# Layers 2 and 3: bonus and level 0 in one product set, narrow tiles for levels 4 and 5, the 512 to 160 projection token by token

## The chip, the cores and the metric

The kernel runs on one core of a Trainium2 chip. The metric is the device time of one execution in microseconds, lower is better; a time shown without more is the median of several executions. Engines are named as in the profile: PE (TensorE), PEld (its weight loads), DVE (VectorE), ACT (ScalarE), POOL (GpSimd), SP (SyncE, which only issues transfers here).

## The reference

Four cross-attention layers run one after the other over 16 batch items of 128 tokens with 512 channels, all in float32. Layer 0 is attention with 64 inner channels, layer 1 a latent attention with an MLP of 2048, layer 2 a block of the RWKV kind, layer 3 grouped-query attention with a layer norm. The change is in layers 2 and 3, nearly all of it in the first half of layer 2:

```python
xa = _ln(x, ln1_w, ln1_b)
sx = shifted(xa) - xa
xxx = jnp.tanh((xa + sx * maa_x) @ maa_w1).reshape(b, l, 5, DM)      # 512 -> 160
xxx = jnp.einsum('blfd,fde->blfe', xxx, maa_w2)
xm = xa[:, :, None] + sx[:, :, None] * (maa_stack + xxx)             # five mixes: k, w, v, r, g
w = jnp.exp(-jnp.exp(time_decay + jnp.tanh(xw @ td_w1) @ td_w2))
r, k, v, g = xr @ Wr.T, xk @ Wk.T, xv @ Wv.T, silu(xg @ Wg.T)
def step(s, rkvw):                     # one head: 16 x 16 state, 32 heads, token by token
    a = k_t[..., :, None] * v_t[..., None, :]
    out = jnp.einsum('bhi,bhij->bhj', r_t, u * a + s)                # u: the bonus
    s = a + w_t[..., :, None] * s
```

## The kernel before

Each layer is written engine by engine, with semaphores set by hand. Layers 2 and 3 are `layers23`. The work on one batch item is cut into five stages, n, p, w, a and b (first layer norm; the recurrence; the rest of layer 2; attention; last layer norm), and in one turn of the loop each stage works on another item, so that a turn holds one item's work of every stage. `ORDER` lists, for each engine, the steps of a turn in the order in which that engine takes them: an engine goes through its list strictly, and a step whose semaphore isn't there yet holds all that is behind it. The first four turns and the last four run with part of the stages. TensorE's list is unrolled, the others are loops. The engines' steps have the same names; on TensorE `p_mix` multiplies, on ScalarE, VectorE and GpSimd `p_xm` finishes each mix.

The recurrence is done in levels. The scores between a token and the tokens before it are built by doubling: for the level `lv` with n = 2^lv, the tokens of an odd block of n meet the keys of the even block ahead of it. `p_diag` makes the products of each token with itself, with the bonus u in `ur` (L1433). `p_level(lv)` (L1624 to L1643) makes the level's products: for 4 channel chunks, 2 halves of the tokens and 4 row groups of 32 channels (two heads) one matmul with K2 (64 keys, each with an even-head and an odd-head column, so 128 weight columns) as weights and 32 tokens of rT as moved operand. Every float32 matmul is two records in the profile, a transpose one. VectorE merges the level into AD under a mask (`p_merge`, L2095) and multiplies the odd tokens of rT by their decay (`p_rup`, L2085), GpSimd multiplies the even keys (`p_kup`, L1445), both with the products of decays that `p_wl` made. Each level claims the four banks "quad", which the merge before it frees, and waits for its rup and kup. `p_s0`, `p_av` and `p_av6` then weigh the values.

The projection from 512 to 160 (`p_t5`, L1541 and L1543) has the channels of maa_w1 as weights and 128 tokens moved: four matmuls for the first 128 outputs, four for the other 32. Its tanh (t5, t5b) feeds `p_mix` (L1555, four mixes, each on its own row group and bank of quad) and `p_mix4` (L1564, the fifth, on row group 0, into bank 7). `p_g` leaves tanh and value in two tiles; `out` has a tile of its own.

PSUM banks are claimed through `Use`: a step on TensorE waits until the step before it on that bank has been emptied. `USES` says which step has which bank (quad, 5, 6 or 7).

Of the kernel before, what the change touches and what calls it, by code (L numbers as in the profile page):

```python
# [447 lines left out]
def layer1(nc, a, PS, sem, C, R, cols_of, ident, halfs, bn_scale, bn_shift, l0_out, l1_out, weights, early,  # L448
# [15 lines left out]
    with ExitStack() as ctx:  # L464
# [63 lines left out]
        with nc.Block() as block:  # L528
            @block.sync
            def _(sp):  # L530
# [526 lines left out]
def layers23(nc, a, PS, quad, sem, C, R, CS, col_at, ident, hsum, halfs, l1_out, early, s_early):  # L1057
# [6 lines left out]
    SETUP = 12  # L1064
    LAT = [0, 32, 48, 56, 60, 62]
    NLM = 64

    with ExitStack() as ctx:
# [6 lines left out]
        def chunked(t):  # L1075
# [23 lines left out]
        t5 = sb("t5", [P, P])  # L1099
        t5b = sb("t5b", [DM, P])  # L1100
# [4 lines left out]
        ur = sb("r_bonus", [P, NC, P])  # L1105
# [5 lines left out]
        AD6 = xmix[:, 0:2, :, :].rearrange("p f c t -> p (f c t)").rearrange("p (n t) -> p n t", t=HALF)  # L1111
# [3 lines left out]
        zg = sb("gate_tanh", [P, D])  # L1115
# [42 lines left out]
        out = sb("out3", [P, D])  # L1158
        wvm = out[:, 0:P].rearrange("p (c m h) -> p c m h", c=NC, m=NC)
# [36 lines left out]
        s_gate = sem("p_silu_ready")  # L1196
# [29 lines left out]
        USES = {("n_xa",): (6, 1), ("p_t5",): (6, 1), ("p_mix",): ("quad", RG), ("p_mix4",): (7, 1), ("p_u1",): (5, 1), ("p_w",):  # L1226
                (6, 1), ("p_k",): (5, 1), ("p_r",): (6, 1), ("p_v",): (5, 1), ("p_g",): (7, 1), ("p_diag",): ("quad", 1),
                ("p_level", 0): ("quad", 1), ("p_level", 1): ("quad", 1), ("p_level", 2): ("quad", 1), ("p_level", 3): ("quad", 1),
                ("p_level", 4): ("quad", 1), ("p_level", 5): ("quad", 1), ("p_level", 6): ("quad", 1), ("p_s0",): (7, 1),
                ("w_var",): (7, 1), ("w_rstd",): (6, 1), ("w_out",): (7, 1), ("w_xc",): (6, 1), ("w_fk",): (6, 1), ("w_fr",): (7,  # L1230
                1), ("w_fv",): (5, 1), ("a_x",): (5, 1), ("a_q",): (5, 1), ("a_kv",): (6, 1), ("a_score", 0): ("quad", RG),
                ("a_score", 1): ("quad", RG), ("a_turn", 0): (6, 1), ("a_turn", 1): (5, 1), ("a_turn", 2): (5, 1), ("a_turn", 3):
                (6, 1), ("a_turn", 4): (6, 1), ("a_turn", 5): (7, 1), ("a_turn", 6): (5, 1), ("a_turn", 7): (5, 1), ("a_norm",): (7,
                1), ("b_out",): (7, 1)}
# [3 lines left out]
            pe=[("p_t5",), ("a_x",), ("w_var",), ("p_mix",), ("a_kv",), ("b_out",), ("a_q",), ("p_mix4",), ("w_rstd",), ("a_score",  # L1238
                0), ("p_k",), ("p_r",), ("a_score", 1), ("p_u1",), ("a_turn", 0), ("w_out",), ("a_turn", 1), ("p_w",), ("p_diag",),
                ("a_turn", 2), ("p_g",), ("p_level", 0), ("w_xc",), ("p_v",), ("a_turn", 3), ("p_level", 1), ("w_fr",), ("p_level",  # L1240
                2), ("n_xa",), ("a_value", 0), ("a_turn", 6), ("p_level", 3), ("w_fk",), ("p_level", 4), ("a_turn", 5), ("a_turn",
                7), ("a_turn", 4), ("a_norm",), ("p_level", 5), ("w_fv",), ("p_level", 6), ("a_value", 1), ("p_s0",), ("p_av",),
                ("p_av6",)],
            act=[("p_t5",), ("a_x",), ("p_xm", 0), ("p_xm", 3), ("p_xm", 1), ("a_kv",), ("p_xm", 2), ("a_q",), ("w_rstd",), ("p_xm",
                 4), ("p_k",), ("a_exp", 0), ("p_r",), ("a_exp", 1), ("p_u1",), ("a_exp", 2), ("a_turn", 0), ("a_turn", 1),
                 ("a_exp", 3), ("a_turn", 2), ("p_w",), ("p_g",), ("w_xc",), ("a_exp", 6), ("a_exp", 5), ("a_turn", 3), ("p_v",),
                 ("a_exp", 4), ("a_exp", 7), ("n_xa",), ("w_fr",), ("a_turn", 6), ("w_fk",), ("a_turn", 5), ("a_turn", 7),
                 ("a_turn", 4), ("a_norm",), ("b_store",), ("p_level6",), ("a_bias",), ("p_wkv",)],
# [1148 lines left out]
```

## Time and profile before

| | |
|---|---|
| median of 3 runs | 2489.3 us (2488.08 to 2489.41) |
| the profiled execution, its time | 2494.95 us |
| its span, first to last instruction | 2492.6 us |
| mean granted TensorE clock | 0.966 |
| busy | PE 2331.0, PEld 1720.1, DVE 1111.1, ACT 1082.6, POOL 552.4 us |
| layers 0 and 1 | until about 1200 us |
| layers 2 and 3 | from about 1200 us on |

Busy times are from one execution. PE's count the tail of each matmul, so they say who is full, not how near the engine is to its peak; what a group of matmuls costs is read from its start and the start of the next group.

### The profile page before, as it was taken

Reading aid. Unit: us, or ns where it says so; the run is one execution under the profiler, and the core shown is the slowest. Engines: PE = TensorE matmul, PEld = TensorE weight load, DVE = VectorE, ACT = ScalarE, POOL = GpSimd, SP = SyncE. Lnnn points to the kernel's source line nnn. Section 1 sums busy time; section 2 is a strip of 40 time slices with the busy share of each in tenths; the row PEclk is TensorE's granted clock in tenths of the full one; section 3 lists DMA queues with packets and bytes.
Section 4 is the critical chain, followed back from the end, with each engine's and each line's share of the span. In section 5 each row is a group of like instructions: output and inputs, shape, how many; then the busy total and the mean of one; then the engine's idle time right before and its main releaser. Section 6 shows DMA issues by size and latency. Waiting matters only on the chain. (4 is left out here: it accounts for less than half of the span.)

```text
span 2492.6 us, 59022 instructions
## 1 busy us (share of the span) xinstructions
PE 2331.0 (94%) x22880; PEld 1720.1 (69%) x22880; DVE 1111.1 (45%) x3070; ACT 1082.6 (43%) x3409; POOL 552.4 (22%) x585
## 2 busy tenths in 40 slices
PE   7886999999999999999488999999999999999986
PEld 3444667777777666667276878777777877777864
DVE  5662222222222222222234565655666655665542
ACT  4552333333333333333112655555555455555544
POOL 0001010110000000000023334333333343343320
PEclk9997999999999999999678999999999999999998
DMA  5421000000000000000600000111000011100010
GB/s 165 168 89 65 15 18 18 22 18 18 18 18 18 18 18 18 18 10 5 191 15 16 21 17 14 25 25 25 20 20 12 23 25 25 25 20 16 10 25 14
DMA packets 117056, 81.93 MB, mean 33 GB/s; under 512 B 79136, under 2 KB 91680, under 8 KB 114720
## 3 DMA queue, kind: packets, MB, share of 16 engines
q1 hardware_dynamic: 107744, 54.32, 8.2%
q0 software_dynamic: 2240, 12.58, 1.5%
q10 hardware_dynamic: 6912, 12.59, 1.3%
q8 instruction: 138, 2.26, 0.4%
q14 instruction: 22, 0.18, 0.0%
HBM read 62.68 MB, written 12.58 MB: 30 GB/s over the span
## 5 line engine op out<-in xcount | busy, mean ns | idle before, releaser
L745 PEld LDWEIGHTS bank<-normedT,mlp_w 128*128 128x128 f32 x2048 | 235.7, 193 | 18.3 <-issue 17.1
L745 PE MATMUL bank<-normedT,mlp_w 128*128 128x128 f32 x2048 | 241.7, 278 | 0.8 <-DVE normedT L975 0.8
L755 PE MATMUL bank<-mlp_w,geluT 128*128 128x512 f32 x512 | 228.9, 595 | 0.0
L1638 PEld LDWEIGHTS quad<-rT,k_even_odd 32*128 32x128 f32 x6144 | 187.2, 193 | 39.5 <-DVE wkv_scores L2095 29.7
L926 DVE CUSTOM_DVE_ANT_0 probs<-quad,neg_mask 128x256 f32<-128x256 f32 x256 | 90.8, 421 | 273.8 <-PE quad L675 273.8
L1638 PE MATMUL quad<-rT,k_even_odd 32*128 32x32 f32 x6144 | 197.9, 278 | 13.9 <-DVE wkv_scores L2095 11.5
L2095 DVE COPY_PREDICATED wkv_scores<-level_masks,quad 128x1024 f32<-128x1024 int32 x96 | 160.6, 1673 | 93.4 <-PE quad L1638 93.4
L1930 ACT ACTIVATE scores<-scores,nmax 128x128 f32<-128x128 f32 x512 | 198.9, 400 | 2.9 <-DVE nmax L2185 2.9
L933 DVE COPY probsT<-quad 128x512 f32<-128x512 f32 x128 | 84.9, 683 | 191.9 <-PE quad L689 191.7
L755 PEld LDWEIGHTS bank<-mlp_w,geluT 128*128 128x128 f32 x512 | 93.6, 190 | 103.4 <-issue 103.4
L1445 POOL TENSOR_TENSOR k_even_odd<-k_even_odd,decay_products 128x512 f32<-128x512 f32 x80 | 95.9, 1199 | 275.9 <-PE quad L1638 275.9
L861 ACT ACTIVATE geluT<-bank,cols 128x128 f32<-128x128 f32 x256 | 73.3, 369 | 178.2 <-PE bank L745 178.2
L2085 DVE TENSOR_TENSOR rT<-rT,decay_products 128x256 f32<-128x256 f32 x96 | 61.9, 645 | 160.4 <-PE quad L1638 123.4
L869 ACT ACTIVATE probs<-probs,nmax 128x256 f32<-128x256 f32 x256 | 126.6, 498 | 2.6 <-DVE nmax L926 2.4
L1386 POOL TENSOR_TENSOR gn_rstd<-gn_var_eps,halfs 128x32 f32<-128x32 f32 x16 | 87.1, 5443 | 159.1 <-DVE gn_var_eps L2110 159.1
L2185 DVE CUSTOM_DVE_ANT_0 scores<-quad,mask 128x128 f32<-128x128 f32 x512 | 112.7, 287 | 21.5 <-PE quad L1748 20.8
L1402 POOL TENSOR_TENSOR xm<-xm,xaT 128x512 f32<-128x512 f32 x80 | 101.1, 1264 | 77.4 <-DVE xm L2053 77.4
L647 PE MATMUL quad<-hT,k_w 128*128 128x256 f32 x512 | 113.2, 379 | 0.0
L656 PE MATMUL quad<-v_w,hT 128*128 128x512 f32 x256 | 112.5, 592 | 0.0
L579 POOL COPY rinv_repeated<-rinv 128x256 f32<-128x256 f32 x32 | 12.8, 399 | 439.2 <-DVE rinv L939 439.2
L1939 ACT ACTIVATE probsT<-bank 128x512 f32<-128x512 f32 x128 | 73.0, 597 | 75.6 <-PE bank L1505 75.6
L647 PEld LDWEIGHTS quad<-hT,k_w 128*128 128x128 f32 x512 | 96.1, 190 | 12.4
(238 smaller groups left out, 4463.7 us busy)
## 6 DMA issues: line engine op xcount, KB each, us to landing
x_in<-in_x SPq DMA_DIRECT2D x32, 256.0 KB, 3.0
mlp_w<-in_mlp_w POOLq DMA_DIRECT2D x8, 1024.0 KB, 5.5
ctx_in<-in_ctx SPq DMA_DIRECT2D x16, 256.0 KB, 2.9
l_out<-wy ACTq DMA_DIRECT2D x16, 256.0 KB, 2.2
wy_in<-l_out SPq DMA_DIRECT2D x16, 256.0 KB, 3.4
hT<-in_ctxT SPq DMA_DIRECT2D x16, 256.0 KB, 3.5
l_out<-l_x ACTq DMA_DIRECT2D x16, 256.0 KB, 2.0
x_in<-l_out SPq DMA_DIRECT2D x16, 256.0 KB, 3.0
```

The costliest lines, as they stand in the source:

```text
L647: mm = nc.tensor.matmul(PS[b][:, e * 256:(e + 1) * 256], k_w[:, c, m * P:(m + 1) * P], hT[:, c, :], start=(c == 0), stop=(c == NC - 1))
L656: mm = nc.tensor.matmul(PS[b][:, :], hT[:, c, n * P:(n + 1) * P], v_w[:, c, :], start=(c == 0), stop=(c == NC - 1))
L745: mm = nc.tensor.matmul(PS[b][:, f * P:(f + 1) * P], mlp_w1[:, c, m * P:(m + 1) * P], nT[:, c, :], start=(c == 0), stop=(c == NC - 1))
L755: mm = nc.tensor.matmul(PS[M.bank][:, :], gT[:, f, :], mlp_w2[:, f, :], start=(f == 0), stop=(f == NF - 1))
L869: ac = nc.scalar.activation(probs[:, h, :], probs[:, h, :], ACT.Exp, bias=nmax[:, h:h + 1], scale=-1.0, accum_out=rsum[:, h:h + 1])
L926: mx = nc.vector.tensor_tensor_reduce(probs[:, h, :], PS[b][:, e * 256:(e + 1) * 256], negm[:, :], -1.0 / D1, 3.0e38, ALU.add, ALU.min, nm ...
L1402: nc.gpsimd.tensor_tensor(xmix[:, f, :, :], xmix[:, f, :, :], xaT[:, :, 1:P + 1], ALU.add)\
L1445: nc.gpsimd.tensor_tensor(k, k, w.unsqueeze(2).to_broadcast([P, D // (2 * n), 2 * n]), ALU.mult)\
L1638: mm = nc.tensor.matmul(PS[r][:, at:at + SB], keys(rr, c, s), odd, start=True, stop=True)
L1930: ac = nc.scalar.activation(s, s, ACT.Exp, bias=nmax[:, k, 2 * c + e:2 * c + e + 1], scale=-1.0, accum_out=rsum[:, kv, gr:gr + 1])
L2095: nc.vector.copy_predicated(AD[:, :, :].rearrange("p q (n two w) -> p q n two w", two=2, w=n)[:, :, :, 1, :], lm[:, at:at + m].unsqueeze(1 ...
L2185: op = nc.vector.tensor_tensor_reduce(sc[k][:, c, e, :], PS[k % RG][:, at:at + P], mask[:, :], -1.0, 3.0e38, ALU.add, ALU.min, nmax[:, k, ...
```

## The change

- **One set for bonus and level 0.** `p_diag` is gone on TensorE and VectorE. A second key tile K0 holds the keys with the odd tokens multiplied by u (`p_k0`, GpSimd), a second r tile `rm` has the even tokens multiplied by u; level 0 multiplies K0 by all 64 tokens of rm, and one merge with a mask of its own takes the diagonal and the pairs. rT and K2 are no longer read by level 0, so `p_rup` 0 and `p_kup` 0 don't wait for it.
- **Levels 4 and 5 with narrow tiles.** Level 5 has 32 keys (64 weight columns) and writes 64 partitions; level 4 has two blocks of 16 keys (32 weight columns) and 16 tokens each, so twice the matmuls. Level 5 is merged by a plain copy of 64 partitions.
- **The projection token by token.** z's tokens are the weights and the 160 outputs are moved: four matmuls. The tanh is in t5, with the last 32 outputs four times; `p_t5t` transposes both halves and ScalarE copies them to t5T. `p_mix4` uses the four copies on four row groups and writes the four banks of quad.
- **k in its own buffer.** K0 also takes the place of xm as AD6, the scores of level 6.
- `p_g` writes the tanh alone, and `p_gate` multiplies from PSUM. `out` lies in scores 3, so `a_max` 3 waits for the store. maa_w2b has 128 columns and is loaded in four pieces. `p_k` on ScalarE has four pieces of half the size.
- `USES` and the five lists of `ORDER` are new.

```diff
...
+        USES = {("n_xa",): (7, 1), ("p_t5",): (6, 1), ("p_t5t",): (6, 1), ("p_mix",): ("quad", RG), ("p_mix4",): ("quad", 1),
...
+            pe=[("p_t5",), ("a_x",), ("w_var",), ("p_t5t",), ("b_out",), ("p_mix",), ("a_q",), ("a_kv",), ("p_mix4",), ("p_k",),
+                ("w_rstd",), ("a_score", 0), ("p_u1",), ("p_r",), ("a_score", 1), ("p_w",), ("w_out",), ("a_turn", 0), ("p_level",
+                0), ("p_g",), ("a_turn", 2), ("p_level", 1), ("w_xc",), ("p_v",), ("a_turn", 3), ("p_level", 2), ("a_turn", 1),
+                ("n_xa",), ("w_fr",), ("p_level", 3), ("w_fk",), ("p_level", 4), ("a_turn", 4), ("a_value", 0), ("a_turn", 7),
+                ("a_turn", 5), ("p_level", 5), ("a_turn", 6), ("w_fv",), ("p_level", 6), ("a_norm",), ("a_value", 1), ("p_s0",),
+                ("p_av",), ("p_av6",)],
+            act=[("p_t5",), ("a_x",), ("p_t5t",), ("p_xm", 0), ("p_xm", 1), ("p_xm", 3), ("p_xm", 2), ("a_q",), ("a_kv",), ("p_xm",
+                 4), ("b_store",), ("p_k",), ("w_rstd",), ("p_u1",), ("a_exp", 0), ("p_r",), ("a_exp", 2), ("p_w",), ("a_exp", 3),
+                 ("a_exp", 1), ("p_g",), ("a_turn", 0), ("a_turn", 2), ("w_xc",), ("p_v",), ("a_turn", 3), ("a_exp", 6), ("n_xa",),
+                 ("a_exp", 4), ("a_turn", 1), ("a_exp", 7), ("w_fr",), ("a_exp", 5), ("w_fk",), ("a_turn", 4), ("a_turn", 7),
+                 ("a_turn", 6), ("a_turn", 5), ("p_level6",), ("a_norm",), ("a_bias",), ("p_wkv",)],
+            dve=[("n_ln1",), ("w_var",), ("b_out",), ("p_xm", 0), ("p_s0c",), ("p_xm", 3), ("p_xm", 1), ("b_ln",), ("p_xm", 4),
+                 ("w_rstd",), ("a_max", 0), ("a_max", 2), ("a_max", 1), ("a_max", 3), ("p_xm", 2), ("w_gate",), ("a_max", 6),
+                 ("a_max", 5), ("a_max", 4), ("a_max", 7), ("p_rup", 0), ("w_out",), ("p_merge", 0), ("n_nx",), ("w_ln2",),
+                 ("p_gate",), ("p_merge", 1), ("p_rup", 1), ("w_sx",), ("w_xr",), ("w_xk",), ("p_merge", 2), ("p_rup", 2), ("p_rup",
+                 3), ("p_merge", 3), ("n_shift",), ("a_rinv",), ("p_rup", 4), ("p_merge", 4), ("p_rup", 5), ("p_merge", 5),
                  ("p_rup", 6), ("w_fv",), ("a_norm",)],
+            pool=[("w_pow",), ("b_rstd",), ("p_xm", 0), ("w_rep",), ("n_rstd",), ("p_xm", 3), ("n_first",), ("p_xm", 1), ("p_xm",
+                  4), ("p_k0",), ("a_x3b",), ("w_first",), ("p_xm", 2), ("p_ur",), ("p_wl",), ("p_kup", 0), ("w_rstd2",), ("p_kup",
+                  1), ("p_kup", 2), ("p_kup", 3), ("p_s0b",), ("p_kup", 4), ("a_norm",), ("p_kup", 5)],
+            sp=[("n_ldx",), ("w_lda",), ("n_lds0",), ("p_v",), ("p_ldw",)])
...
                 def p_k0(i, uses):
+                    pool.wait_ge(u.free, u.done)
+                    nc.gpsimd.tensor_tensor(odd[0], odd[1], CS("u")...to_broadcast([P, NC, HALF, 2]), ALU.mult).then_inc(s_k0, 1)
...
                 def p_t5(i, uses):
-                        nc.tensor.matmul(PS[b][:, 0:P], maa_w1[:, c, 0:P], z[:, c, :], start=(c == 0), stop=(c == NC - 1))
-                    for c in range(NC):
-                        mm = nc.tensor.matmul(PS[b][0:DM, P:2 * P], maa_w1[:, c, P:P + DM], z[:, c, :],
+                        mm = nc.tensor.matmul(PS[b][:, 0:NM * DM], z[:, c, :], maa_w1[:, c, :], start=(c == 0), stop=(c == NC - 1))
...
+                def p_t5t(i, uses):
+                    pe.wait_ge(s_t5, i + 1)
+                    for k in range(2):
+                        mm = nc.tensor.transpose(PS[b][:, k * P:(k + 1) * P], t5[:, k * P:(k + 1) * P], ident[:, :])
...
                 def p_mix4(i, uses):
-                        mm = nc.tensor.matmul(PS[b][:, m * P:(m + 1) * P], maa_w2b[0:DM, m * P:(m + 1) * P], t5b[:, :],
+                        r = slice(DM * m, DM * m + DM)
+                        mm = nc.tensor.matmul(PS[m][:, 0:P], maa_w2b[r, :], t5T[r, P:2 * P], start=True, stop=True)
...
                 def p_level(i, uses, lv):
+                    if lv == 0:
+                        pe.wait_ge(s_k0, i + 1)
+                        pe.wait_ge(s_ur, i + 1)
...
+                                    if lv == 0:
+                                        mm = nc.tensor.matmul(PS[r][:, at:at + HALF], keys(K0, rr, c, s), rm[rr, c, s:s + HALF],
...
+                            elif lv < 6:
+                                for b in range(SB // n):
+                                    for r in range(RG):
+                                        rr, s = slice(SB * r, SB * r + SB), HALF * bh + 2 * n * b
+                                        mm = nc.tensor.matmul(PS[r][4 * n * b:4 * n * b + 2 * n, at + n * b:at + n * b + n],
+                                                              keys(K2, rr, c, s, n), rT[rr, c, s + n:s + 2 * n], start=True, stop=True)
...
                 def p_merge(i, uses, lv):
+                    else:
+                        op = nc.vector.tensor_copy(AD[0:HALF, :, SB:HALF], grid[0:HALF, :, 0:SB])
...
                 def a_max(i, uses, k):
+                    if k == 3 and later(i):
+                        dve.wait_ge(s_store, 16 * i + 16)
```

## Rows read from the trace of the kernel before

**Rows 1.** The page, its first line: the span.

```profile
span 2492.6 us, 59022 instructions
```

**Rows 2.** Busy time by stretch: one turn; busy us and instructions, granted clock, DMA share, GB/s.

```profile
1500.00:1573.35 73.35, 73.03 (x999) 57.96 (x998) 44.36 (x123) 40.06 (x135) 28.07 (x29) 1.00 0.09 21
```

**Rows 3.** Timeline of PE, parts of one level: start, us spanned, instructions.

```profile
1700.94 0.40 PE L1638 MATMUL quad<-rT,k_even_odd 32*128 32x32 f32 x5
...
1700.94 0.42 PE L1638 MATMUL quad<-rT,k_even_odd 32*128 32x32 f32 x8
```

**Rows 4.** Timeline of PE over one turn, same columns.

```profile
1735.63 1.10 PE L1666 MATMUL bank<-wkv_scores,v_even_odd 128*32 128x64 f32 x64
1736.54 0.63 PE L1674 MATMUL bank<-xm,v_even_odd 128*32 128x64 f32 x32
1737.10 1.16 PE L1541 MATMUL bank<-z,maa_w 128*128 128x128 f32 x8
1738.19 1.06 PE L1543 MATMUL bank<-z,maa_w 128*32 128x128 f32 x8
1739.18 0.66 PE L1505 MATMUL bank<-ident,x 128*128 128x128 f32 x4
1739.68 0.96 PE L1684 MATMUL bank<-hsum,gn_squares 128*128 128x8 f32 x8
1740.56 1.17 PE L1555 MATMUL quad<-t,maa_w 32*128 32x128 f32 x32
1741.67 1.16 PE L1734 MATMUL bank<-ctxT,Wk 128*128 128x128 f32 x8
...
1743.55 3.60 PE L1518 MATMUL bank<-Wo,attnT 128*128 128x512 f32 x8
1746.99 3.73 PE L1512 MATMUL bank<-ffn_k_in,Wq 128*128 128x128 f32 x32
1750.65 1.15 PE L1564 MATMUL bank<-t5b,maa_w2b 32*128 32x128 f32 x8
1751.74 0.33 PE L1693 MATMUL bank<-ident,gn_squares 128*128 128x128 f32 x1
...
1768.19 2.01 PE L1620 MATMUL quad<-r_bonus,k_even_odd 32*128 32x64 f32 x64
1770.13 0.66 PE L1505 MATMUL bank<-ident,scores 128*128 128x128 f32 x4
...
1774.29 1.99 PE L1638 MATMUL quad<-rT,k_even_odd 32*128 32x32 f32 x64
1776.21 0.66 PE L1505 MATMUL bank<-ident,gn_dev 128*128 128x128 f32 x4
```

**Rows 5.** Waits of PE, 1410 to 2355 us: in total, times, longest.

```profile
PE quad L1638 <- DVE wkv_scores L2095: 3.5, 11, 0.3
```

**Rows 6.** Weight loads by shape, 1400 to 2350 us: busy us, mean ns of one.

```profile
L1638 PEld LDWEIGHTS quad<-rT,k_even_odd 32*128 32x128 f32 x4992 | 146.3, 186 | 23.8 <-DVE wkv_scores L2095 16.3 <-issue 4.4
...
L1666 PEld LDWEIGHTS bank<-wkv_scores,v_even_odd 128*32 128x32 f32 x832 | 12.2, 110 | 1.6
L1573 PEld LDWEIGHTS bank<-xm,td_w 128*64 128x64 f32 x104 | 11.0, 136 | 4.3 <-issue 4.3
```

**Rows 7.** Timeline of POOL: p_ur.

```profile
1761.52 1.04 POOL L1433 TENSOR_TENSOR r_bonus<-rT,cols 128x512 f32<-128x512 f32 x1 [0.98 <-ACT rT L1840]
```

**Rows 8.** Timeline of ACT: p_xm 0, 3 and 1, then 2.

```profile
1741.80 3.22 ACT L1815 ACTIVATE xm<-quad,cols 128x128 f32<-128x128 f32 x12 [1.33 <-PE quad L1555]
...
1745.72 1.26 ACT L1815 ACTIVATE xm<-quad,cols 128x128 f32<-128x128 f32 x4
```

**Rows 9.** Timeline of DVE: merge of level 1, then rup and merge of level 4.

```profile
1784.12 2.43 DVE L2095 COPY_PREDICATED wkv_scores<-level_masks,quad 128x1024 f32<-128x1024 int32 x1
...
1798.44 0.42 DVE L2085 TENSOR_TENSOR rT<-rT,decay_products 128x256 f32<-128x256 f32 x1 [3.31 <-PE quad L1638]
1798.78 1.32 DVE L2095 COPY_PREDICATED wkv_scores<-level_masks,quad 128x1024 f32<-128x1024 int32 x1
```

More of the change, by code:

```diff
@@ L1223, in layers23 @@
         S = {k: (sem(f"l23_{k}_psum_ready"), sem(f"l23_{k}_psum_free")) for k in ("quad", 5, 6, 7)}
-        USES = {("n_xa",): (6, 1), ("p_t5",): (6, 1), ("p_mix",): ("quad", RG), ("p_mix4",): (7, 1), ("p_u1",): (5, 1), ("p_w",):
-                (6, 1), ("p_k",): (5, 1), ("p_r",): (6, 1), ("p_v",): (5, 1), ("p_g",): (7, 1), ("p_diag",): ("quad", 1),
+        USES = {("n_xa",): (7, 1), ("p_t5",): (6, 1), ("p_t5t",): (6, 1), ("p_mix",): ("quad", RG), ("p_mix4",): ("quad", 1),
+                ("p_u1",): (6, 1), ("p_w",): (6, 1), ("p_k",): (7, 1), ("p_r",): (5, 1), ("p_v",): (7, 1), ("p_g",): (6, 1),
@@ L1232, in layers23 @@
-                ("a_score", 1): ("quad", RG), ("a_turn", 0): (6, 1), ("a_turn", 1): (5, 1), ("a_turn", 2): (5, 1), ("a_turn", 3):
-                (6, 1), ("a_turn", 4): (6, 1), ("a_turn", 5): (7, 1), ("a_turn", 6): (5, 1), ("a_turn", 7): (5, 1), ("a_norm",): (7,
-                1), ("b_out",): (7, 1)}
+                ("w_var",): (7, 1), ("w_rstd",): (5, 1), ("w_out",): (7, 1), ("w_xc",): (5, 1), ("w_fk",): (7, 1), ("w_fr",): (5,
+                1), ("w_fv",): (6, 1), ("a_x",): (5, 1), ("a_q",): (6, 1), ("a_kv",): (5, 1), ("a_score", 0): ("quad", RG),
@@ L1235, in layers23 @@
+                ("a_score", 1): ("quad", RG), ("a_turn", 0): (5, 1), ("a_turn", 1): (6, 1), ("a_turn", 2): (7, 1), ("a_turn", 3):
+                (6, 1), ("a_turn", 4): (5, 1), ("a_turn", 5): (7, 1), ("a_turn", 6): (5, 1), ("a_turn", 7): (6, 1), ("a_norm",): (5,
+                1), ("b_out",): (5, 1)}
         BANK = {(k[0] if len(k) == 1 else k): bank for k, (bank, _) in USES.items()}
         ORDER = dict(
[L1238 to L1248, printed above, removed]
@@ L1559, in p_mix4 @@
                 def p_mix4(i, uses):
-                    u, b, t = uses[("p_mix4",)], BANK["p_mix4"], uses[("p_t5",)]
+                    u, t = uses[("p_mix4",)], uses[("p_t5t",)]
                     claim(u)
@@ L1955, in b_store @@
                     act.dma_start(a["out"][i], out[:, :]).then_inc(s_store, 16)
-                steps(act, "act", dict(n_xa=n_xa, p_t5=p_t5, p_xm=p_xm, p_u1=p_u1, p_w=p_w, p_k=p_k, p_r=p_r, p_v=p_v, p_g=p_g,
+                steps(act, "act", dict(n_xa=n_xa, p_t5=p_t5, p_t5t=p_t5t, p_xm=p_xm, p_u1=p_u1, p_w=p_w, p_k=p_k, p_r=p_r, p_v=p_v, p_g=p_g,
                                        p_level6=p_level6, p_wkv=p_wkv, w_rstd=w_rstd, w_xc=w_xc, w_fk=w_fk, w_fr=w_fr,
@@ L1979, in _ @@
                 dve.wait_ge(s_setup, n_setup)
-                for lv in range(6):
+                for lv in range(1, 5):
                     at, m = LAT[lv], HALF // 2 >> lv
```

202 lines of the change are left out of this document (106 added, 96 removed).

## Prediction

> **What bounds the kernel now.** I read the page first for the span, then the busy time by stretch, the waits of TensorE, its instructions in order of time over one turn, and last the other engines over the same turn. The span is 2492.6 us [rows 1], the time of that execution 2494.95 us, and the median of the runs 2489.3 us: 5.65 us lower, which I take off at the end. In a full turn of the loop of layers 2 and 3 TensorE is busy 73.03 of 73.35 us at full granted clock (the 1.00 in the row, the 2.4 GHz level), VectorE 44.36, ScalarE 40.06, GpSimd 28.07 [rows 2]. The turn is 73.35 us long: the same product set starts at 1700.94 [rows 3] and at 1774.29 [rows 4]. TensorE waits for one thing in thirteen such turns, 3.5 us in all for the merge of a level, so some 0.3 us a turn [rows 5]. So each microsecond of TensorE's issue taken from a turn shortens it by one, sixteen times over, as long as nobody else becomes late. All prices are differences between starts of consecutive groups, because matmuls overlap and the durations count the tail.
>
> **The change, part by part (TensorE, one turn).**
>
> *Bonus and level 0 in one set.* The set of p_diag goes: 64 records from 1768.19 to 1770.13 are 1.94 us. The merged set has 64 columns moved where level 0 had 32; the old diag set has just that shape and costs 1.94, level 0 costs 1.92 (1774.29 to 1776.21) [rows 4]. So **-1.9**.
>
> *512 to 160 projection.* Old: 1737.10 to 1738.19 for the first 128 outputs and to 1739.18 for the other 32, together 2.08. New: 8 records with 160 columns. A record of 512 columns costs 3.44/8 = 0.43 us (1743.55 to 1746.99), so 0.84 ns a column, 0.134 us for 160, 1.08 for eight; the 128-column group has 1.09 where this gives 0.86, so 0.23 is fixed: 1.31. Two transposes come on top; four take 0.50 (1739.18 to 1739.68), two 0.27. **-0.5** [rows 4]. The path p_t5, tanh, transposes, copy, p_mix gets longer, but p_t5t stands behind a_x and w_var, and p_mix behind b_out (3.44 us), which cover it. With that cover gone it would be some 1.5 us.
>
> *The fifth mix on four row groups (p_mix4).* Old: 8 records on one row group, 1750.65 to 1751.74, 1.09. New: two fours in four banks. p_mix is 32 records, eight fours, in 1.11 (1740.56 to 1741.67); without the 0.23 a four is 0.11, two 0.22, with it 0.45. **-0.6** [rows 4], with 0.3 and 0.8 as bounds.
>
> *Level 5 with 64 weight columns.* In a level the records go out in fours, one on each row group, some 7 ns apart: five matmuls of the set span 0.40 us and eight 0.42 [rows 3]. 1.92 us for sixteen fours is 0.12 a four, and it is the same for 32 and for 64 moved columns, so the moving side does not set it. The weight load does: 186 ns for 128 columns, 136 for 64, 110 for 32 [rows 6]. A load 50 ns shorter gives 0.07 a four, 1.1 in all; the value product (32 weight columns, 64 moved) does 64 records in 0.91 (1735.63 to 1736.54) [rows 4]. I take 1.0: **-0.9**, bounds 0 and -1.0.
>
> *Level 4 as 32x32 tiles.* Twice the records: 128 in 32 fours. From below 7 ns each, 0.9 us; at the value product's 14.2 ns each 1.8; at the unchanged 0.12 a four 3.84. Loads 76 ns shorter give 0.044 a four, 1.4. I take 1.3, near the load, since the moved side has only 16 columns here: **-0.6**, bounds -1.0 and +1.9.
>
> *The rule that speaks against it.* The Trainium skill, "TensorE: Matmul & The Clock Gate", section "Wait — 56ns, not 53.3ns?", says that matmuls start no closer than about 25 ns however small they are. By that (an estimate) level 4 would take 3.2 us and level 5 1.6, and the turn would save only about 2.4. The trace here disagrees where tiles run side by side: 64 records in 0.91 us are 14.2 ns each [rows 4].
>
> *The wait.* The 0.3 us are at level 2, behind w_fr alone; in the new order a_turn 1, n_xa and w_fr stand ahead of level 3, and w_xc, p_v and a_turn 3 ahead of level 2: **-0.3**.
>
> Sum: 1.9 + 0.5 + 0.6 + 0.9 + 0.6 + 0.3 = 4.8 us a turn, 73.35 to about 68.5.
>
> **What lies beside TensorE.** VectorE loses a masked merge of 2.4 us and its level 5 becomes a copy: off the path, nothing. ScalarE gets p_t5t and two more pieces in p_k and loses the second copy of p_g; GpSimd gets p_k0, a 512-wide product like the r_bonus one of 1.04 us [rows 7]. With 33 and 45 us idle in a turn [rows 2] these cost nothing by volume; what counts is order. Where an order is tight I compared the work that TensorE has in between with the work that must be done:
> - p_mix4 now claims the four quad banks, so ScalarE must have emptied them: twelve pieces in 3.22 us and four in 1.26 [rows 8], 4.5 in all. TensorE has a_q (3.66) and a_kv (1.88) meanwhile, 5.5 [rows 4]. Slack 0.9. Behind it are queued p_k and all that p_k feeds.
> - a_score 0 needs the quad back from p_xm 4, with a_q and a_kv ahead of it on ScalarE: some 2.4 us of copies after a_kv against p_mix4, p_k and w_rstd, 4.7. Slack 2.3.
> - level 1 to 2: the merge of 2.43 [rows 9] and a rup, 0.42 there and, if it stretches beside GpSimd as far as it could, some 1.4 (an estimate), 3.8, against w_xc (0.5), p_v (3.44) and a_turn 3 (0.5). Slack 0.6; the old gap was w_fr alone, which is where the 0.3 came from.
> - level 4 to 5: rup and merge end 1.8 us after the level [rows 9]; TensorE has a_turn 4, a_value 0, a_turn 7, a_turn 5, 2.5. Slack 0.6.
> - level 0 needs p_ur: 1.1 us of GpSimd and 0.6 of ScalarE after p_r, against a_score 1, p_w, w_out and a_turn 0, 6 us.
> - the p_wl and p_kup 0 chain no longer waits for level 0, and p_rup 0 neither: earlier than before.
> - the SP queue now begins with n_ldx, which waits for n_nx behind merge 0; w_lda, n_lds0, p_v and p_ldw stand behind it. p_v waits for its copy later than that anyway, and its four transfers have the levels 2 to 6 to land.
> - out3 now lies in scores 3: a_max 3 waits for the store, which is issued some 3 us ahead of it.
>
> The whole: 16 x 4.8 = 77 us. In the first batch the other stages are not there yet to fill TensorE, so the projection's longer chain (the 1.5 us above) lies bare and a shorter set only means a longer wait for the merge. I take 3 us off, a guess of that size: 74. 2494.95 - 74 = 2421, less 5.65: **2415 us**.
>
> **Rivals.**
> 1. *A new wait gives part back.* The slacks of 0.6 to 0.9 us are thin, and a merge with GpSimd beside it took 2.43 where another took 1.32 [rows 9]. If the merge ahead of level 5 takes the long one, level 5 waits 0.5; two or three such waits are 1 to 2.5 us a turn, 16 to 40 us: 2431 to 2455. For it: thin slacks. Against: the three tight places have more work between them than before, and only one place waited before.
> 2. *A small record costs what a large one does.* If 30 ns a record (1.92/64) hold whatever the width, level 4 takes 3.84 and level 5 stays: the turn saves 4.8 - 0.9 - 0.6 - 1.9 = 1.4, in all 22 us: 2467. Against: the 14.2 ns. The skill's 25 ns would give about 2452.
> 3. *Slower: level 0 waits for the bonus on GpSimd.* p_ur now stands behind p_k0, a_x3b, w_first and p_xm 2, and p_xm 2 behind VectorE's eight maxima and the store. If this chain comes late, TensorE stands at level 0, and from there every stage. It decides the sign from the point where level 0 starts 5 us late, so p_ur must be some 9 us later than it looks (4.3 slack + 4.8). The chain ahead of it is four operations of 1 to 1.6 us, so this is unlikely.
>
> **How the numbers follow.** Forecast 0.76; rival 1 0.15; rival 2 0.05; rival 3 0.03; 0.01 that it comes out even. The forecast's own range: level 4 and 5 at the value product's rate add 0.5 us a turn (+8 us), mix4 at its bounds 0.2, small waits 0.3 a turn (+5); on the other side level 4 at 0.9 and level 5 at 0.9 take off another 0.5 a turn (-8), edges 3: 2402 to 2431. The range reaches into rival 1: **2398 to 2443**. A change below 0.2% (5 us) can't be told from none here. Faster 0.96 (forecast and rivals 1 and 2), same 0.01, slower 0.03.
>
> **What would show it.** In the changed kernel's trace: turns of 68 to 69 us; TensorE busy above 99% of a turn; the level 0 set 1.9 us; level 5 about 1.0 and level 4 between 0.9 and 1.9 from start to next start; p_t5 1.3 and two transposes 0.3; p_mix4 0.45; no wait at p_mix4 for ScalarE's xm. Wrong if level 4 takes over 2 us, if TensorE waits over 1 us a turn for wkv_scores, xm or r_bonus, or if the clock falls in a turn.

## The result, and the profile after

The changed kernel takes **2411.12 us** (median of 4 runs, 2409.21 to 2411.85); the kernel before 2489.36 us, now the median of 4. The ratio is 0.9685, 95% interval 0.9668 to 0.9701: 78.2 us or 3.2% less. The forecast was 2415 us, with 2398 to 2443 as its range. The profiled execution took 2411.85 us, only 0.7 above the median, where that of before lay 5.65 above its own.

The first line of the page after, which answers to [rows 1]:

```profile
span 2410.1 us, 58947 instructions
```

Busy time over one full turn, which answers to [rows 2] (PE, PEld, DVE, ACT, POOL, granted clock, DMA share, GB/s):

```profile
1500.00:1568.80 68.80, 68.47 (x992) 53.37 (x991) 42.15 (x122) 40.35 (x139) 29.34 (x30) 1.00 0.10 22
```

TensorE is as full as before (68.47 of 68.80 us), at full clock, and nobody else came near it. The turn is 68.81 us: p_mix starts at 1700.64 and again at 1769.45. Seven of the twelve full turns are that long within 0.05; the slowest three, one behind the other, are 70.06, 69.05 and 69.15. Its timeline, which answers to [rows 4]:

```profile
1700.64 1.17 PE L1578 MATMUL quad<-t5T,maa_w 32*128 32x128 f32 x32
...
1707.30 0.50 PE L1589 MATMUL quad<-t5T,maa_w2b 32*128 32x128 f32 x8
1707.73 3.84 PE L1529 MATMUL bank<-xm,Wk 128*128 128x128 f32 x32
...
1723.83 2.01 PE L1653 MATMUL quad<-r_bonus_even,k_bonus_odd 32*128 32x64 f32 x64
1725.78 3.84 PE L1529 MATMUL bank<-xm,Wg 128*128 128x128 f32 x32
...
1748.42 1.42 PE L1662 MATMUL quad<-rT,k_even_odd 32*32 32x16 f32 x128
1749.77 0.66 PE L1522 MATMUL bank<-ident,scores 128*128 128x128 f32 x4
...
1752.38 1.13 PE L1662 MATMUL quad<-rT,k_even_odd 32*64 32x32 f32 x64
1753.44 0.66 PE L1522 MATMUL bank<-ident,scores 128*128 128x128 f32 x4
...
1762.67 1.35 PE L1558 MATMUL bank<-maa_w,z 128*128 128x160 f32 x8
1763.86 0.60 PE L1522 MATMUL bank<-ident,x 128*128 128x128 f32 x4
...
1765.12 0.41 PE L1567 MATMUL bank<-ident,t 128*128 128x128 f32 x2
1765.85 3.67 PE L1535 MATMUL bank<-Wo,attnT 128*128 128x512 f32 x8 [0.32 <-ACT ffn_k_in L1936]
...
1769.45 1.17 PE L1578 MATMUL quad<-t5T,maa_w 32*128 32x128 f32 x32
```

Read as differences between starts: the merged set 1.95 us, level 4 1.35, level 5 1.06, the fifth mix 0.43, p_t5 1.19, the two transposes 0.73 with a wait of 0.32 in it. Before, the same work took 1.94 + 1.92 (bonus and level 0), 1.92, 1.92, 1.09 and, for the whole projection, 2.08. Level 4 takes 1.32 to 1.37 in all full turns. Level 5 takes 1.06 in most, but 1.30 and 1.38 in the turns of 69.05 and 69.15; no run says why.

The waits of TensorE, 1410 to 2270 us, which answer to [rows 5] (total, times, longest):

```profile
PE bank L1535 <- ACT ffn_k_in L1936: 3.2, 10, 0.3
PE bank L1522 <- issue: 1.2, 1, 1.2
```

The old wait for the merge is gone. A new one of the same size stands at b_out, and once TensorE waits 1.2 us for nothing that the profile names (from 1820.24 us, in the turn of 70.06). ScalarE empties a_x's bank with

```profile
1765.11 0.60 ACT L1936 ACTIVATE ffn_k_in<-bank 128x512 f32<-128x512 f32 x1 [0.18 <-ACT t L1835]
```

that is until 1765.71, and b_out starts at 1765.85.

The weight loads by shape, which answer to [rows 6]:

```profile
L1662 PEld LDWEIGHTS quad<-rT,k_even_odd 32*32 32x32 f32 x1664 | 16.7, 103 | 2.0
L1662 PEld LDWEIGHTS quad<-rT,k_even_odd 32*64 32x64 f32 x832 | 13.6, 132 | 2.4 <-issue 2.3
```

And VectorE behind level 4, which answers to [rows 9]:

```profile
1750.10 0.42 DVE L2116 TENSOR_TENSOR rT<-rT,decay_products 128x256 f32<-128x256 f32 x1 [0.94 <-PE quad L1662]
1750.44 1.30 DVE L2133 COPY_PREDICATED wkv_scores<-level_masks,quad 128x1024 f32<-128x1024 int32 x1
```

The merge ends at 1751.74, level 5 starts at 1752.38: the 0.6 us of slack that the prediction counted.

**Where the 82.5 us of the two spans lie.** Three stretches of the kernel before, from the first transposes of layer 2 to the first three batches' value products:

```profile
1226.50:1300.20 73.70, 52.55 (x672) 46.89 (x672) 27.26 (x39) 16.69 (x44) 18.61 (x21) 0.66 0.27 92
1300.20:1372.70 72.50, 64.18 (x839) 51.42 (x838) 31.31 (x47) 19.87 (x52) 25.10 (x25) 0.85 0.06 14
1372.70:1442.20 69.50, 69.50 (x989) 56.43 (x988) 39.04 (x117) 39.33 (x134) 26.77 (x27) 1.00 0.09 19
```

and the same three of the changed kernel:

```profile
1223.30:1287.30 64.00, 43.40 (x668) 37.87 (x668) 25.55 (x38) 17.30 (x46) 20.48 (x22) 0.69 0.30 103
1287.30:1352.00 64.70, 57.30 (x834) 45.06 (x833) 29.05 (x46) 20.39 (x54) 26.74 (x26) 0.87 0.08 15
1352.00:1417.40 65.40, 64.83 (x983) 51.96 (x982) 37.23 (x117) 39.85 (x137) 28.90 (x28) 1.00 0.11 20
```

They are 9.7, 7.8 and 4.1 us shorter, 21.6 together, 8 more than three full turns save (4.5 us each). Layers 0 and 1, which the change doesn't touch, came out 3.2 us shorter in this execution (1226.5 against 1223.3), and what is left, 2492.6 - 1442.2 = 1050.4 against 2410.1 - 1417.4 = 992.7, is 57.7 us for the remaining thirteen batches.

### The profile page after: what moved, and what is told of

Read it like the earlier page. It is cut to its first block, busy times and chain, and to the rows that moved or that the text cites. A ratio compares the mean times of both kernels' runs of the same rounds, so it can differ in the third digit from the quotient of the medians.

```text
span 2410.1 us, 58947 instructions
## 1 busy us (share of the span) xinstructions
PE 2248.5 (93%) x22784; PEld 1639.6 (68%) x22784; DVE 1079.0 (45%) x3056; ACT 1087.0 (45%) x3441; POOL 574.7 (24%) x601
## 4 chain that ended last, share of the span: by engine, by line
PE 45%; ACT 2%; issue 2%; DVE 1%; POOL 0%; ACTq 0%; POOLq 0%; DVEq 0%
PE bank L1529 13%; PE bank L1535 12%; PE quad L1657 4%; PE bank L1522 4%; PE quad L1662 2%; PE quad L1774 1%; PE bank L1790 1%; PE quad L1653 1%; PE quad L1578 1%; PE bank L1680 1%; PE quad L1667 1%; PE bank L1692 1%; PE bank L1597 1%; PE bank L1605 1%; PE bank L1762 1%
## 5 line engine op out<-in xcount | busy, mean ns | idle before, releaser
L746 PEld LDWEIGHTS bank<-normedT,mlp_w 128*128 128x128 f32 x2048 | 234.9, 193 | 18.1 <-issue 17.1
L2116 DVE TENSOR_TENSOR rT<-rT,decay_products 128x256 f32<-128x256 f32 x96 | 41.0, 427 | 175.8 <-PE quad L1657 70.5
L1849 ACT ACTIVATE xm<-quad,cols 128x128 f32<-128x128 f32 x320 | 86.2, 411 | 67.1 <-PE quad L1578 65.2
L2133 DVE COPY_PREDICATED wkv_scores<-level_masks,quad 128x1024 f32<-128x1024 int32 x64 | 100.3, 1567 | 32.3 <-PE quad L1657 32.3
L1657 PEld LDWEIGHTS quad<-rT,k_even_odd 32*128 32x128 f32 x3072 | 90.1, 187 | 19.3 <-issue 17.5
L1963 ACT ACTIVATION_READ_ACCUMULATOR scores<-scores,nmax 128x1 f32 x512 | 100.6, 196 | 0.0
```

What stands on the lines that cost most here:

```text
L746: mm = nc.tensor.matmul(PS[b][:, f * P:(f + 1) * P], mlp_w1[:, c, m * P:(m + 1) * P], nT[:, c, :], start=(c == 0), stop=(c == NC - 1))
L1657: mm = nc.tensor.matmul(PS[r][:, at:at + SB], keys(K2, rr, c, s), odd, start=True, stop=True)
L1963: ac = nc.scalar.activation(s, s, ACT.Exp, bias=nmax[:, k, 2 * c + e:2 * c + e + 1], scale=-1.0, accum_out=rsum[:, kv, gr:gr + 1])
L2133: op = nc.vector.copy_predicated(AD[:, :, :].rearrange("p q (n two w) -> p q n two w", two=2, w=n)[:, :, :, 1, :], lm[:, at:at + m].unsque ...
```

## The experiments

Each is the changed kernel with the edit shown, but for e7, which starts from the kernel before. Times are medians; "before" stands for the kernel before in the same set of runs (2490.64, 2490.15 and 2490.94 us in the three sets). e1 to e4 ran on another chip than the control; that the kernel before came out within 0.8 us in all three sets says how far off a difference from the control can be by this.

**e12, the control.** The changed kernel again, in the set of e9 to e11.

> The changed kernel itself, on the same chip as the three others, as their control: 2411 us, within 2.

2410.72 us (2408.58 to 2412.55), ratio 0.9676 (0.9662 to 0.9689). Five runs lie 4 us apart, so a difference of 2 us between two kernels says nothing.

**e1, b_out in another bank.**

```diff
-                1), ("b_out",): (5, 1)}
+                1), ("b_out",): (7, 1)}
```

> The changed kernel with b_out in bank 7 in place of bank 5, nothing else. Theory A (the 0.32 us for which TensorE waits ahead of b_out in each turn is the claim on bank 5, which ScalarE empties of a_x only at 1765.7): the wait goes, no other comes, turns of 68.5 us in place of 68.8, 16 x 0.3 = 4 to 5 us less than the changed kernel, about 2406.5. Rival B (the gap is not the bank but ScalarE as such: the next step p_mix waits for t5T behind it, or b_out waits for attnT): the gap moves or stays, same time within 1 us.

2408.08 us (2405.67 to 2410.18), ratio 0.9666 (0.9653 to 0.9679). In the trace the wait is gone, and the only one left between 1410 and 2270 us is

```profile
PE bank L1522 <- issue: 1.2, 1, 1.2
```

So the wait was the claim on bank 5, which a_x still held: theory A on the cause. Turns went from 68.81 to 68.57. From the start of the two transposes to that of b_out it is 0.52 us in place of 0.73, where the changed kernel has 0.41 to 0.43 in the turns in which it does not wait: some 0.1 us of another wait is left, too short for the list. The time is 2.6 us below the control of another set and inside the scatter, so the gain in time is not shown.

**e2, level 4 with 128 weight columns.**

```diff
-                            if lv < 4:
+                            if lv < 5:
```

> The changed kernel with level 4 in 128 weight columns and 64 records again; levels 5 and 0 as changed. Theory A (the set's time follows the width of the weight load, 1.35 us narrow, 1.92 wide): turns 0.57 longer, 16 x 0.57 = 9 us more, about 2420. Rival B (twice the records use up what the narrow load saves once the sets around them overlap, or the wait at level 5 hides it): under 3 us.

2417.96 us, ratio 0.9707 (0.9692 to 0.9721): 7 more than the control, where the width alone asks for 9. The set is 1.92 us again (1755.04 to 1756.96), and the full turns are 69.38, 0.57 longer. The missing 2 us are the 1.2 for which TensorE waited in the changed kernel and the 0.6 of the two longer turns behind it, which are not there. But neither are they in e4, whose level 4 is narrow: the width alone does not bring that wait (see e6 and e9). Theory A, with its size off by 2 us.

```profile
1755.04 1.99 PE L1657 MATMUL quad<-rT,k_even_odd 32*128 32x32 f32 x64
1756.96 0.66 PE L1522 MATMUL bank<-ident,scores 128*128 128x128 f32 x4
```

**e3, level 5 with 128 weight columns.**

```diff
-                            if lv < 4:
+                            if lv < 4 or lv == 5:
```

> The changed kernel with level 5 in 128 weight columns again. Theory A: the set 1.92 in place of 1.06 us, turns 0.86 longer, 14 us more, about 2425; in the first batch, where TensorE waits for the merges, less than that. Rival B (the old price of the set was the 64 records, not the weights): no change.

2424.66 us, ratio 0.9737 (0.9722 to 0.9752): 13.9 more than the control. Theory A, to the microsecond (turns of 69.67, 0.86 longer); 64 records in both cases, so it was not their number.

**e4, level 0's products twice.**

```diff
-                    for c in range(NC):
+                    for c in (*range(NC), *range(NC)) if lv == 0 else range(NC):
```

> The changed kernel with the products of level 0 made twice, so that TensorE again has eight sets a batch, while VectorE has seven merges. Theory A (what the merged set saves is TensorE's 1.94 us, nothing else): 16 x 1.94 = 31 us more, about 2442, in the first batches as much as in the full turns. Rival B (part of the gain came from the missing merge of 2.4 us or from the waits around it): less than 25 us more, because a longer set hides under other waits in the first batches.

2435.02 us, ratio 0.9778 (0.9763 to 0.9793): 24.3 more than the control, under the 25 that rival B set as its bound, not 31. Two things in the trace. The second set costs 1.78 and not 1.94, since it follows its like without the fixed part at the change of group:

```profile
1732.60 3.80 PE L1653 MATMUL quad<-r_bonus_even,k_bonus_odd 32*128 32x64 f32 x128
1736.33 3.84 PE L1529 MATMUL bank<-xm,Wg 128*128 128x128 f32 x32
```

(3.73 us for both, against 1.95 for one.) That is 2.5 us over sixteen batches. Full turns are 70.6, longer by just this 1.78. Of the 4 us that are left, some 3 are in the first two turns, which are 61.5 and 63.6 us long here and 60.8 and 63.7 in the changed kernel, though they hold the second set too; the wait of 1.2 us is not there either. So rival B's number came true, and its reason for some 3 us of it; nothing here shows a gain from the merge that VectorE no longer has.

**e5, the fifth mix on one row group.**

```diff
                         r = slice(DM * m, DM * m + DM)
+                        r = slice(0, DM)
                         mm = nc.tensor.matmul(PS[m][:, 0:P], maa_w2b[r, :], t5T[r, P:2 * P], start=True, stop=True)
```

> The changed kernel with all four matmuls of the fifth mix on row group 0 (it leaves out three quarters of that mix's weights: each of the four takes the first piece, so the values of the gate differ). Theory A (four row groups side by side are the gain): p_mix4 1.09 in place of 0.43 us, 16 x 0.65 = 10 us more, about 2421. Rival B (the matmuls were held by their four banks or by the claim on quad): no change.

2420.75 us, ratio 0.972 (0.9703 to 0.9736): 10.0 more than the control. p_mix4 takes 1.08 (1709.00 to 1710.08), still in four banks: the row groups are the gain. Theory A.

```profile
1709.00 1.15 PE L1590 MATMUL quad<-t5T,maa_w2b 32*128 32x128 f32 x8
1710.08 3.84 PE L1529 MATMUL bank<-xm,Wk 128*128 128x128 f32 x32
```

**e6, level 3 narrow too.**

```diff
-                            if lv < 4:
+                            if lv < 3:
```

> The changed kernel with level 3 cut as levels 4 and 5 are: four blocks of 8 keys, 16 weight columns, 8 tokens moved, 256 records. Theory A (records of narrow tiles are limited by their issue, 7 ns each, as within a four): 1.8 to 2.0 us, the time stays within 2 us of 2411. Rival B (a four of narrow records has a floor of 42 ns, the 1.35/32 of level 4, whatever the width): 64 fours are 2.7 us, turns 0.8 longer, 12 us more, about 2423.

2470.21 us (2461.13 to 2476.31), ratio 0.991 (0.9887 to 0.9933): 59 us *more* than the control. Neither theory had that. The timeline of one turn:

```profile
1769.86 1.56 PE L1662 MATMUL quad<-rT,k_even_odd 32*16 32x8 f32 x171
1773.82 0.86 PE L1662 MATMUL quad<-rT,k_even_odd 32*16 32x8 f32 x85 [2.41 <-issue]
1774.62 6.66 PE L1529 MATMUL bank<-ffn_k_in,Wfk 128*128 128x128 f32 x32
1781.21 1.26 PE L1662 MATMUL quad<-rT,k_even_odd 32*32 32x16 f32 x128
```

The records themselves are fast: 171 in 1.56 us, about 8 ns each once the 0.25 of the last one's length is off (theory A). But then TensorE stands still for 2.4 us inside the set with nothing in the profile to wait for, and the product behind it, 3.8 us otherwise, takes 6.6. The stretches say why the second:

```profile
1769.80:1774.60 4.80, 2.39 (x257) 2.23 (x256) 0.00 (x0) 3.88 (x18) 0.00 (x0) 0.91 0.01 3
1774.60:1781.20 6.60, 6.60 (x42) 6.47 (x32) 4.32 (x8) 0.00 (x0) 2.32 (x2) 0.55 0.24 30
1781.20:1786.00 4.80, 4.80 (x221) 3.85 (x220) 1.65 (x2) 2.38 (x4) 1.85 (x2) 1.00 0.28 31
```

The granted clock is 0.55 over w_fk, nearly all of it at the lower of the two levels (0.50, 1.2 GHz), and 1.00 again behind it. Full turns are 71 to 75 us, 2 to 6 longer than in the changed kernel.

**e9, level 4 twice, with its 32-column tiles: is it the tile or the number?**

```diff
-                                for b in range(SB // n):
+                                for b in (*range(SB // n), *range(SB // n)) if lv == 4 else range(SB // n):
```

> The changed kernel with level 4's narrow products made twice: 256 records of 32x32 tiles in one row, as many as level 3 had in 16-column tiles, where the time rose by 59 us with a stall of 2.4 us inside the set and a lower granted clock behind it. Theory A (so many short records in a row run the engine out of instructions, whatever the tile): the same stall after some 170 records, clock below full in the turns, 40 to 60 us more. Rival B (the 16-column tiles or the 8 moved tokens did it): the set simply takes 2.5 to 2.7 us, 16 x 1.2 = 20 us more, clock at full.

2496.89 us (2492.88 to 2499.25), ratio 1.0025 (1.0015 to 1.0034): 86 more than the control and slower than the kernel before. The picture is that of e6 with the tiles of level 4, so it does not take the 16-column tiles. Theory A, but not in its size: the stall comes here after 254 records of the set, not 170, and costs more than its 40 to 60 us. A turn is 75.0 us, 6.2 longer: the set takes some 5.2 from start to next start in place of 1.35, and the rest is work behind it at the lower clock.

```profile
1702.27 1.40 PE L1662 MATMUL quad<-rT,k_even_odd 32*32 32x16 f32 x128 [0.22 <-issue]
1706.29 0.28 PE L1662 MATMUL quad<-rT,k_even_odd 32*32 32x16 f32 x2 [2.62 <-issue]
1706.50 1.11 PE L1522 MATMUL bank<-ident,scores 128*128 128x128 f32 x4
```

with the clock

```profile
1703.70:1706.30 2.60, 0.01 (x1) 0.02 (x1) 0.00 (x0) 0.00 (x0) 0.00 (x0) 0.63 0.50 54
1706.30:1709.00 2.70, 2.70 (x22) 1.47 (x22) 1.62 (x2) 0.00 (x0) 1.85 (x2) 0.50 0.02 6
```

Between 1410 and 2270 us there are ten such stalls at this set, of 2.0 to 2.6 us (with an eleventh wait of 0.2, the 23.8 us that the profile gives for it), and one of 1.1 two groups behind it. In e6 there are nine of 2.1 to 2.8 and one of 1.0 at level 3. In every one of them, and in the single one of the changed kernel, the list of transfers has a packet of the "instruction" queue, 16 KB, that begins within 1.7 us of the last record and lands about 1 us later, and TensorE goes on 1.3 to 1.6 us behind its landing. The one of e9 above, 1703.4 to 1706.3 us, by queue (packets, MB, share):

```profile
q1 hardware_dynamic: 2356, 0.15, 50.6%
q8 instruction: 1, 0.02, 2.3%
```

The transfers of the other queue beside it are not needed for the stall. In e6 the instruction packet moved alone, from 1771.32 to 1772.33 us, and from 1771.42 to 1773.82, while TensorE stood still for 2.41 us, no packet began:

```profile
DMA packets 0, 0.00 MB, mean 0 GB/s; under 512 B 0, under 2 KB 0, under 8 KB 0
```

The Trainium skill, "Runtime: NRT & Kernel Launch", section "Instruction fetch mechanics", says that an engine's instructions arrive in blocks of 16 KiB, 256 instructions, fetched while it executes, and that this fetch stays hidden because instructions are dispatched slower than they come. The trace agrees on the size of the packet: a float32 matmul is four instructions (two loads, two matmuls), a turn of the kernel before has some 2000, and the instruction queue moves eight packets of 16 KB in it. It does not agree on the hiding: here 256 records, 512 instructions, went out in 2.8 us of work, and TensorE stood still. That it waits for the fetch is read from these times, which agree within 0.3 us in all the stalls; no run here changed the fetch alone, and why one stall comes after 171 records and another after 254 stays open.

**e7, the narrow tiles alone, in the kernel before.**

```diff
+                        if lv in (4, 5):
+                            for bh in range(2):
+                                at = HALF * (2 * c + bh)
+                                for b in range(SB // n):
+                                    for r in range(RG):
+                                        rr, s = slice(SB * r, SB * r + SB), HALF * bh + 2 * n * b
+                                        mm = nc.tensor.matmul(PS[r][4 * n * b:4 * n * b + 2 * n, at + n * b:at + n * b + n],
+                                                              K2[rr, c, s:s + n, :].rearrange("p s e -> p (s e)"),
+                                                              rT[rr, c, s + n:s + 2 * n], start=True, stop=True)
-                        if lv < 6:
+                        elif lv < 6:
```

> The kernel before with the narrow tiles of levels 4 and 5 alone. Theory A (the parts add up, each by its own set): turns 1.43 shorter in steady state, 16 x 1.43 = 23 us less than before, about 2466, a little more or less in the first batches. Rival B (in the old order the gap between levels 4 and 5, 2.0 us for a chain of 1.85, is too short once level 4 ends sooner): a wait of some tenths appears ahead of level 5 and the gain is under 18 us.

2473.66 us (2466.12 to 2475.92), ratio 0.9926 (0.9909 to 0.9942): 16.5 less than before, not 23. Rival B had the size right and the reason wrong: no wait stands at level 5. Ordinary turns are 71.8 us, 1.6 shorter, where theory A has 1.4, but two of them are 76.5. One of the two:

```profile
1701.29 1.54 PE L1773 MATMUL bank<-probsT,v 128*32 128x256 f32 x16
1702.76 1.12 PE L1505 MATMUL bank<-ident,scores 128*128 128x128 f32 x4
1703.80 3.64 PE L1647 MATMUL quad<-rT,k_even_odd 32*128 32x32 f32 x64
1707.37 6.03 PE L1512 MATMUL bank<-ffn_k_in,Wfk 128*128 128x128 f32 x32
```

TensorE is not idle there, nor in the 2.5 us ahead of it, and still level 3 takes 3.57 in place of 1.92 and w_fk 5.96 in place of 3.77. The granted clock was 0.56 over 1701 to 1707 us. What ran just ahead, behind a wait of 0.32, was level 2, four transposes of n_xa and a_value, all of them small work. The other turns have the same groups in the same order at full clock, so these rows do not say why it fell in two. In the first batch level 4 has the stall of e6 and e9, 2.28 us after 126 of its 128 records. The four times of this kernel lie 10 us apart (2466.12 to 2475.92).

**e8, level 4 with its blocks innermost.**

```diff
-                                for b in range(SB // n):
-                                    for r in range(RG):
+                                for r in range(RG):
+                                    for b in range(SB // n):
```

> The changed kernel with the two blocks of level 4 innermost: the records go to one row group's two tiles in turn and then to the next row group. Theory A (all eight tiles of 32x32 are free for each other, a record costs what its issue costs): the set stays at 1.35 us, the time within 2 us of 2411. Rival B (what runs side by side is one record for each row group, the tiles of one row group take turns): the set takes longer, up to twice, 1 to 1.4 us a turn, 16 to 22 us more.

2411.09 us, ratio 0.9684 (0.9668 to 0.9701), the same as the changed kernel. The set takes 1.27 us in one turn (1747.31 to 1748.58) and 1.32 to 1.38 in all the other full turns, as in the changed kernel. Theory A: two tiles of one row group do not stand in each other's way. The order gains nothing either, so the 0.08 us that the expectation of e11 below counts for it comes from a single turn and is not there.

**e10 and e11, what is left to gain.** e11 is e1 and e8 together; e10 is e11 with

```diff
-("a_kv",), ("p_mix4",), ("p_k",), ("w_rstd",), ("a_score", 0), ("p_u1",), ("p_r",),
+("a_kv",), ("p_k",), ("p_mix4",), ("w_rstd",), ("p_u1",), ("a_score", 0), ("p_r",),
```

> The changed kernel with b_out in bank 7 and with level 4's two blocks innermost. Theory A (both small gains of TensorE's turn add: 0.25 from the bank, 0.08 from level 4, whose set took 1.27 in place of 1.35 us in that order): turns of 68.5, about 5 us less than the control, 2406.5. Rival B (the order of the records gives nothing that can be measured): as the bank alone, 3 to 4 us less.

> The kernel of the next run (b_out in bank 7, level 4 with its blocks innermost) with TensorE taking p_k ahead of p_mix4 and p_u1 ahead of a_score 0. In the first two batches TensorE waits 4.3 us at p_mix4 for ScalarE's xm, which in a full turn other work covers. Theory A (p_k fills that wait, since its own input is there before): 3 us less in each of the two batches, 5 to 6 us less than the next run, about 2401. Rival B (the fifth mix comes 4 us later in each full turn, and VectorE, which takes it ahead of w_rstd and the maxima, passes that on to a_score 1 or level 0): a new wait of over 0.5 us a turn, slower than the next run by 8 us or more.

e11: 2410.41 us (2406.29 to 2412.75), ratio 0.9676 (0.9662 to 0.969). e10: 2409.13 us (2407.37 to 2410.56), ratio 0.9671 (0.9657 to 0.9684). Neither can be told from the control. Full turns are 68.57 in e11, as in e1, and 68.68 in e10. In e10 the wait of p_mix4 in the first two batches (8.7 us in e11) has only moved to p_k:

```profile
PE bank L1529 <- issue: 6.1, 1, 6.1
PE bank L1529 <- POOL xm L1406: 5.1, 1, 5.1
```

p_k's own input was not there either, so theory A falls; rival B's new wait in full turns did not come. No version beats the changed kernel by more than these runs can tell.

## Why the prediction was right, point by point

The time lies 4 us below the forecast, and the mechanism is the one forecast: TensorE sets the turn, and each set that was made shorter shortened it. That it comes so near is in part luck: full turns gave 5 us less than forecast and the first batches 9 more (see *The whole*).

| term, us a turn | forecast | trace | by experiment |
|---|---|---|---|
| bonus and level 0 in one set | -1.9 | -1.91 | e4: +24.3 for a second set of 1.78 |
| projection with its transposes | -0.5 | -0.48 without the wait | not tried |
| fifth mix | -0.6 | -0.66 | e5: +10.0 |
| level 5 | -0.9 | -0.86 | e3: +13.9 |
| level 4 | -0.6 | -0.57 | e2: +7 |
| waits | -0.3 | -0.1: the old one -0.4, the new one +0.3 | e1 |
| sum | -4.8 | -4.6; the turns say -4.54 | |

- *Level 4 and 5*: both fell between their bounds, next to what the loads gave. The rule of the Trainium skill, "TensorE: Matmul & The Clock Gate", section "Wait — 56ns, not 53.3ns?", that matmuls start no closer than about 25 ns would have given 3.2 and 1.6 us (an estimate from that figure). The trace disagrees where tiles run side by side: 1.35 and 1.06 us, 10.5 ns a record for level 4, and 8 in e6.
- *The projection*: right in its sum nearly, wrong in both parts. The four matmuls with 160 columns took 1.19 us where 1.31 was forecast (the fixed part of 0.23 was too much), and the two transposes 0.41 where 0.27 was.
- *The wait*: the one step of the turn that failed. The old wait went, as forecast, and a new one ate most of it, 0.3 us a turn. The places "where an order is tight" left out the bank of b_out. In the kernel before, b_out had bank 7 and started 4.4 us behind a_x; `USES` now gives it bank 5, which a_x also has, and it would start 1.7 us behind a_x. ScalarE empties a_x's bank behind the tanh of p_t5 (0.44 us, against 0.42 before), until 1765.71, and b_out cannot start before. Counting the claims of all steps, not only of quad, would have shown it.
- *The slacks*: p_mix4 did not wait in full turns, the slack of level 5 was 0.6, level 2 and level 1 did not wait. Rival 1 (new waits of 1 to 2.5 us) has 0.3 of it.
- *Rival 2* (a price for each record) is refuted by e3, e5 and the set times. *Rival 3* (level 0 waits for the bonus): 1.0 us once, in the first batch.
- *The range*: its lower end of 2402 does not quite follow from the terms named, 2415 - 8 - 3 = 2404 (2401 with the fifth mix at its bound too); the stated range starts at 2398, so nothing hangs on it.
- *The whole*: I took 3 us off for the first batches; between these two executions they gave 8 more than full turns instead. Some 2 of the 8 are not the change. In the profiled execution of before TensorE waited 6.89 us for the first xm, in e7, where this part is the same, 5.08. Layers 0 and 1, also the same, ended 3.1 us earlier in e7, at 1223.45, as in the changed kernel. These 1.8 and 3.1 make up most of the 5.65 by which that execution lay above its median. So the first batches gave some 6 us beyond full turns, 9 more than I had counted, and full turns 0.3 x 16 = 5 less: 4 us net, the 78.2 measured against 74 forecast.

"A shorter set only means a longer wait" failed, mostly because of the clock. In the first batch of the kernel before, level 2 and each level after it ran at the low clock, here levels 2 and 3:

```profile
1273.97 3.64 PE L1638 MATMUL quad<-rT,k_even_odd 32*128 32x32 f32 x64 [2.89 <-DVE wkv_scores L2095]
1279.47 3.64 PE L1638 MATMUL quad<-rT,k_even_odd 32*128 32x32 f32 x64 [0.82 <-DVE rT L2085]
```

in the changed kernel levels 2 and 3 ran at the high one, here level 3:

```profile
1270.62 1.99 PE L1657 MATMUL quad<-rT,k_even_odd 32*128 32x32 f32 x64 [1.28 <-DVE rT L2116]
```

The granted clock was 0.50 for 30.7 us from 1273.5 before, and for 17.1 us from 1272.9 now. Ahead of level 2 TensorE stood 2.89 us before; now p_v lies between levels 1 and 2 and it does not wait there. e7, the old order with the narrow tiles, has that wait (2.88 us) and level 2 at the low clock (3.57 us); in all the runs with the new order level 2 comes at the high one. So this part goes with the rest of the change, the new order in it, and not with the narrow tiles. That it is the missing wait that kept the clock up fits these rows; it was not tested by itself.

## What to carry to other kernels

Where one engine is full in every turn, price each edit by the difference between starts of consecutive groups on that engine, take the shape's nearest row for the new one, and the sum came out within 6% here (4.8 against 4.54). Weight loads of small products cost by their columns: 64 records took 1.92 us with 128 columns and 1.06 with 64, and twice as many with 32 took 1.35. So cut the columns that are masked away later, and spread small contractions over the row groups. But count the instructions too: past some 170 to 250 small records in a row TensorE stood still for 2 to 2.8 us and then ran at half clock, which made a set that by its records costs what it did before (e6, level 3) lengthen the turn by 2 to 6 us. And when a step is moved, write down who holds its PSUM bank, not only who makes its data.

## What the runs showed of the hardware that was not expected

- Bursts of 256 narrow float32 records (512 instructions in 2.3 to 2.8 us) met a stall of 1 to 2.8 us in almost every turn (e6, e9). With 128 of them it came once in twelve turns of the changed kernel (1.2 us, 20 records behind the set) and in the first batch of e7 (2.3 us); behind a set of 64 wide ones no wait without a named cause was over 0.4 us (before, e2).
- Each of these stalls ended 1.3 to 1.6 us after a 16 KB packet of the instruction queue had landed, with other transfers beside it (e9, 50.6% of the time of the transfer engines) or without any (e6).
- After the stalls of over 2 us the granted clock was at 0.50 for 3 to 10 us, which costs as much again: a product of 3.8 us takes 6.6. After the 1.2 us of the changed kernel it stayed at 1.00.
- The clock can fall without TensorE being idle just ahead (e7, 0.56 from 1701 to 1707 us), after a row of small groups; it cost 4.7 us in each of two turns, and the other turns with the same row kept the full clock.
- Records on different 32x32 tiles start 8 to 10.5 ns apart, two tiles of the same row group included (e8).
